# Gate products with the gate weights stationary, in one pipeline over the pairs of a half

## The chip, the cores and the metric

The kernel runs on one core of a Trainium2 chip. The metric is the device time of one execution in microseconds (us); lower is better. Before the change the median of 3 runs is 4451.63 us (4451.18 to 4458.18). The profiled execution took 4446.43 us, of which the span from the first to the last instruction is 4444.5 us. The engines are PE (TensorE), DVE (VectorE), ACT (ScalarE), POOL (GpSimd) and SP (SyncE, which here only issues DMAs).

## The reference

One graph layer on 12,500 nodes of 256 features: layer norm, a graph sum over 200,000 edges, linear attention, then a second layer norm and a top-2 mixture of 8 experts. The change concerns the gate of the last step:

```
x = x + gnn(xn) + mix(xn)                        # xn = layernorm(x)
x_flat = layernorm(x)
gate_logits = x_flat @ Wg + bg + bias            # (12500, 256) @ (256, 8)
topk_vals, topk_idx = top_k(gate_logits, 2)
topk_w = softmax(topk_vals)
h = relu(einsum('td,edh->teh', x_flat, W1) + b1)
y = einsum('teh,ehd->ted', h, W2) + b2
out = x + einsum('ted,te->td', y, combine)       # combine: topk_w at topk_idx
```

## The kernel before, in words

The nodes are 98 blocks of 128 rows (`NB`), handled as 49 pairs of blocks (`PAIRS`). A first stage sorts edges and projects the rows, a second gathers messages and adds them and the attention into `acc`, which stays in SBUF as 128 partitions x 98 blocks x 260 columns. Then comes the gate stage and after it the experts. The order of all work is written out by hand; the engines meet at semaphores.

**Gate stage.** The 49 pairs form 7 turns of 7 pairs (`TURN`, 14 blocks each, `TB`). Turns 0 to 2 are half 0 (21 pairs), turns 3 to 6 are half 1 (28 pairs). SP first stores every turn's rows of `acc` to `out` (`keep`, L578), then loads the experts' weights. For each pair:

- DVE normalises the two blocks in place (`normalise`, L1800). Between pairs it takes the statistics of the next turn's blocks (`block_stats`, L1771, 3 after each of the first four pairs and 2 after the fifth), gathers them (`gather_stats`, L1778 and L1780), and at the end of a turn inverts the standard deviation (`invert_turn`, L1786 to L1794), for which ACT has taken the root (`root`, L994).
- PE transposes the pair in 4 instructions into bank 0 or 1 (`f_transpose`, L1357), ACT copies the result to `fxn_t` (`gate_copies`, L1003), and PE multiplies (`gate`, L1365): the transposed rows are the stationary operand, 128 columns, and the gate weights `wg` are the moving one, 8 columns. The logits of a whole turn, tokens on the partitions, gather in bank 2.
- DVE reads bank 2 once a turn (`read_logits`, L1935), after the second pair of the next turn; PE may start the next turn's first product only when that is done (`s_gate_read`).

PE transposes a pair ahead: the order is transpose j, gate j-1. At a turn's end it does the gate of the last pair before the first transpose of the next turn.

After a half, DVE routes it (`route_half`, L1969 to L2060: best two experts, counts, positions) while PE counts tokens (`count_tokens`, L1386), and POOL then sends each block's rows twice to their experts' lists in DRAM (`send`, L772): 84 indirect DMAs for half 0, beside which half 1 goes through the gate. SP loads the first four units of the experts when half 0's sends have landed (L617). Half 1's sends (112) are issued beside the experts' first units.

**Experts.** Units of 256 rows: transposes (L1409), up (L1422), down (L1435) on PE, ACT and DVE between them, POOL adds the rows to `out` (L783). The second unit's up waits for the routing of half 1.

A float32 product is issued as two matmul instructions, a transpose as one, so a pair has 4 instructions of L1357 and 8 of L1365.

## Time and profile before

| | |
|---|---|
| median of the runs | 4451.63 us (4451.18 to 4458.18, n = 3) |
| profiled execution, its span | 4446.43 us, 4444.5 us |
| busy: PE, PE weight load, DVE, ACT, POOL | 3140.5, 2560.2, 2597.7, 604.6, 2537.1 us |
| mean granted clock of TensorE | 0.821 of full speed (its levels are 0.5 and 1) |
| gate stage (first normalised pair to the end of half 1's routing) | 3327.2 to 3599.8 us |
| gate products L1365, 392 instructions, mean | 349 ns |
| transposes L1357, 196 instructions, mean | 429 ns |

Times in all rows are microseconds from the span's start, but "mean ns". A slice of the page is 111 us. In a timeline row, the first number is the start, the second how long the group took, `x` the number of instructions, and the bracket the idle time of the engine before it with what ended it. "remote" and "issue" stand where the profile does not show what ended it. In the chain of waits each row is a piece of the chain that ended last. Ends of matmuls are modelled. In the stretches, "busy" is within the stretch, and the DMA share is the mean over the 16 DMA engines.

### The profile page before, as it was taken

What the parts mean: (1) busy time and instruction counts of PE and PEld (TensorE: products, weight loads), DVE (VectorE), ACT (ScalarE), POOL (GpSimd) and SP (SyncE); (2) the same over time, 40 slices, a digit from 0 to 9 for tenths busy, and PEclk for the clock granted to TensorE, in tenths of its full rate; (3) what the DMA queues carried; (4) which work ended last, traced back from release to release, by engine and by line L of the source; (5) the groups of instructions that cost most, each with busy time, mean ns of one, the idle gap of its engine ahead of it and who ended that gap; (6) DMA issues with size and microseconds to landing.
All of it is one profiled execution on the core that took longest, in us unless ns stands there. A gap on an engine that the chain in (4) does not pass through costs nothing.

```text
span 4444.5 us, 56780 instructions
## 1 busy us (share of the span) xinstructions
PE 3140.5 (71%) x16504; PEld 2560.2 (58%) x16505; DVE 2597.7 (58%) x6324; ACT 604.6 (14%) x1276; POOL 2537.1 (57%) x2437
## 2 busy tenths in 40 slices
PE   5767665566666666665676666666645379999998
PEld 5756554344545545544555555555535368888887
DVE  8887775444544544545767767667655145444444
ACT  8112221100000000000000000000001112222221
POOL 0057777466666666666666666666642447744444
PEclk9987777778778777778888888888875579999999
DMA  6666664533333333333333333333376235644443
GB/s 191 219 185 193 198 188 132 152 101 101 101 99 102 100 99 101 101 97 110 112 112 108 111 107 112 111 109 113 99 106 199 73 67 120 122 78 72 72 71 57
DMA packets 363112, 522.66 MB, mean 118 GB/s; under 512 B 69240, under 2 KB 282748, under 8 KB 363004
## 3 DMA queue, kind: packets, MB, share of 16 engines
q0 software_dynamic: 130944, 275.64, 25.7%
q1 hardware_dynamic: 181523, 190.28, 14.4%
q10 hardware_dynamic: 50537, 55.32, 4.0%
q8 instruction: 65, 1.06, 0.1%
q14 instruction: 43, 0.35, 0.0%
HBM read 378.21 MB, written 140.28 MB: 117 GB/s over the span
## 4 chain that ended last, share of the span: by engine, by line
PE 30%; another core or an unknown queue 17%; DVE 16%; issue 12%; DVEq 5%; DMA 2%; POOL 0%; ACT 0%; SPq 0%; ACTq 0%; POOLq 0%
PE bank L1422 9%; PE bank L1435 9%; DVE acc L1817 7%; PE bank L1230 6%; DVE select L1810 5%; DVEq L56 2%; PE bank L1333 2%; PE bank L1365 2%; DVEq L1817 1%; DVE relu_kq L1904 1%; PE bank L1409 1%; PE bank L1331 1%; DMA read_back<-lists 1%; PE bank L1357 1%
## 5 line engine op out<-in xcount | busy, mean ns | idle before, releaser
L729 POOL DMA_INDIRECT message<-h_table,gather_stage x1660 | 1583.3, 954 | 928.6 <-issue 505.9
L1817 DVE TENSOR_TENSOR acc<-acc,bank 128x256 f32 x1660 | 697.4, 420 | 880.5 <-remote 636.9
L1230 PE MATMUL bank<-message,select 128*128 128x256 f32 x3320 | 976.6, 449 | 294.5 <-issue 165.1
L1230 PEld LDWEIGHTS bank<-message,select 128*128 128x128 f32 x3320 | 726.2, 227 | 530.7 <-issue 245.7
L689 POOL DMA_INDIRECT lists<-placed,dest_i x300 | 374.3, 1248 | 375.7 <-ACT placed L911 281.2
L783 POOL DMA_INDIRECT out<-acc,row_of x224 | 351.3, 1568 | 341.3 <-DVE acc L2110 266.7
L1810 DVE TENSOR_SCALAR select<-iota_n,gather_stage 128x128 f32<-128x128 f32 x1660 | 467.3, 359 | 3.5
L1236 PE MATMUL bank<-w_cat,xt_in 128*128 128x256 f32 x784 | 257.1, 442 | 229.6 <-issue 228.7
L1422 PE MATMUL bank<-fx_t,acc 128*128 128x256 f32 x1792 | 411.8, 383 | 10.1 <-DVEq L2062 4.7
L1435 PE MATMUL bank<-w,acc 128*128 x1792 | 405.6, 379 | 2.7 <-issue 2.7
L1422 PEld LDWEIGHTS bank<-fx_t,acc 128*128 128x128 f32 x1792 | 344.9, 193 | 59.0 <-DVEq L2062 5.0
L1435 PEld LDWEIGHTS bank<-w,acc 128*128 128x128 f32 x1792 | 331.9, 190 | 43.8 <-issue 3.3
L1236 PEld LDWEIGHTS bank<-w_cat,xt_in 128*128 128x128 f32 x784 | 167.9, 216 | 289.1 <-issue 269.1
L772 POOL DMA_INDIRECT x_sorted<-acc,token_pos x196 | 191.4, 976 | 233.3 <-issue 148.4
L2106 DVE TENSOR_TENSOR acc<-bank,table 128x256 f32<-128x256 f32 x224 | 84.7, 419 | 315.0 <-PE bank L1435 258.6
L1331 PE MATMUL bank<-x_in,ident 128*128 128x256 f32 x196 | 102.7, 624 | 214.1 <-issue 120.9
L2094 DVE TENSOR_SCALAR acc<-bank,table 128x256 f32<-128x256 f32 x448 | 193.5, 478 | 67.2 <-PE bank L1422 43.3
L1331 PEld LDWEIGHTS bank<-x_in,ident 128*128 128x128 f32 x196 | 54.3, 304 | 245.0 <-issue 162.4
L1135 PE MATMUL bank<-hot_w,hot_q 128*128 128x128 bf16 x1575 | 157.3, 264 | 46.3 <-issue 44.7
L985 ACT ACTIVATE exp_kq<-bank 128x512 f32<-128x512 f32 x49 | 29.3, 597 | 1144.3 <-PE bank L1311 818.9
L1135 PEld LDWEIGHTS bank<-hot_w,hot_q 128*128 128x128 bf16 x1575 | 129.7, 121 | 68.6 <-issue 65.6
L963 ACT ACTIVATE exp_kq<-bank 128x512 f32<-128x512 f32 x49 | 29.3, 597 | 1027.0 <-remote 1027.0
(299 smaller groups left out, 3848.8 us busy)
## 6 DMA issues: line engine op xcount, KB each, us to landing
rows<-block_dram SPq DMA_DIRECT2D x75, 514.5 KB
acc<-x_sorted SPq DMA_DIRECT2D x112, 260.0 KB
message<-h_table,gather_stage POOLq DMA_INDIRECT x1660
xt_in<-xt_dram SPq DMA_DIRECT2D x98, 256.0 KB
x_sorted<-blank_rows ACTq DMA_DIRECT2D x42, 390.0 KB
lists<-zeros_list SPq DMA_DIRECT2D x8, 1664.0 KB, 15.4
read_back<-lists SPq DMA_DIRECT2D x13, 1024.0 KB, 5.7
x_sorted<-blank_rows SPq DMA_DIRECT2D x2, 6370.0 KB
```

The source lines that it names most:

```text
L689: pool.indirect_dma_start(out=lists, out_offset=Offset(ap=dest_i[:, c, i:i + 1], axis=0), in_=placed[:, c % 4, i * G8 * PIECES:(i + 1) * G ...
L729: pool.indirect_dma_start(out=message[:, slot % SETS, j, :], out_offset=None, in_=h_table, in_offset=Offset(ap=gather_stage[:, slot, j, 0: ...
L783: pool.indirect_dma_start(out=out, out_offset=Offset(ap=row_of[:, ring, j:j + 1], axis=0), in_=fy[:, slot, j, :], in_offset=None, compute_ ...
L1135: last = nc.tensor.matmul(bank[2 + c % 2][:, 0:P], hot_q[:, c % STEP, g, :], hot_w[:, c % STEP, g, :, :].rearrange("p r w -> p (r w)").bit ...
L1230: last = nc.tensor.matmul(ps, select[:, slot % 2, j, :], message[:, slot % SETS, j, :], start=True, stop=True)
L1236: last = nc.tensor.matmul(ps[:, u * C:(u + 1) * C], xt_in[:, half, k, u * P:(u + 1) * P], w_cat[:, k, cols:cols + C], start=(k == 0), stop ...
L1331: nc.tensor.matmul(bank[6][:, u * C:(u + 1) * C], ident[:, :], x_in[:, half, u, :], start=True, stop=False)
L1422: last = nc.tensor.matmul(bank[2 + 2 * slot + h // 2][:, h % 2 * 2 * P:(h % 2 + 1) * 2 * P], w1_now[:, slot, k * HID + h * P:k * HID + (h ...
L1435: last = nc.tensor.matmul(bank[6 + slot][:, j * C:(j + 1) * C], hid_t[:, slot, k, j * P:(j + 1) * P], w2_flat[:, ds(expert + k * C, C)], s ...
L1810: return V.tensor_scalar(select[:, slot % 2, j, :], iota_n[:, :], gather_stage[:, slot, j, 1:2].bitcast(F32), gather_stage[:, slot, j, 2:3 ...
L1817: added = V.tensor_tensor(to, to, ps, ALU.add)
L2094: last = V.tensor_scalar(hid_t[:, slot, h, :], bank[2 + 2 * slot + h // 2][:, h % 2 * 2 * P:(h % 2 + 1) * 2 * P], table_flat[:, ds(expert ...
```

## The change

The gate product is turned round: the gate weights are stationary (8 columns) and the transposed rows move (256 columns), so that a pair's logits come out with the 8 experts on the partitions, in bank 3 or 6. ACT copies them to the new tile `logit_t` (four buffers), and PE turns them back with two transposes (`gate_back`) into the turn's bank, 2 or 7 in alternation. The pairs of a half form one pipeline on PE: transpose g, product g-1, turn back g-2, without a break at turns. ACT's loops over turns are written out. On DVE the next turn's statistics come after the first three pairs of a turn (5, 5 and 4), the gathering after the third, and the read of the last turn's logits after the fourth pair. ACT takes the root in the third pair of a turn.

```diff
--- before.py
+++ after.py
@@ -288,6 +288,7 @@
         xtile_f = sb("xtile_f", [P, 1], F32, route)
         xtile_i = sb("xtile_i", [P, 2, 1], I32, route)
         fxn_t = sb("fxn_t", [P, 2, KC, 2 * P], F32, route)
+        logit_t = sb("logit_t", [EXPERTS, 4, 2 * P], F32, route)
         newton_turn = sb("newton_turn", [P, TB], F32, route)
         route.close()
 
@@ -379,6 +380,8 @@
         s_table = sem("s_table")
         s_kept = [sem(f"s_kept{i}") for i in range(TURNS)]
         s_fin = sem("s_fin")
+        s_logit_psum = sem("s_logit_psum")
+        s_logit = sem("s_logit")
         s_gate = sem("s_gate")
         s_gate_read = sem("s_gate_read")
         s_route = sem("s_route")
@@ -991,18 +994,28 @@
 
             def root(turn):
                 act.wait_ge(s_var, turn + 1)
-                act.activation(rstd[:, ds(turn * TB, TB)], row_mean[:, ds(turn * TB, TB), 1], ACT.Sqrt,
+                act.activation(rstd[:, turn * TB:turn * TB + TB], row_mean[:, turn * TB:turn * TB + TB, 1], ACT.Sqrt,
                                bias=eps_col[:, :]).then_inc(s_std, 1)
 
-            def gate_copies(turn, first=False, last=False):
-                for j in range(TURN):
-                    g = turn * TURN + j
-                    act.wait_ge(s_xt_psum, g + (PAIRS + 1))
-                    if not first or j > 1:
-                        act.wait_ge(s_gate, g if j == 0 else g - 1)
-                    act.activation(fxn_t[:, j % 2, :, :].rearrange("p k n -> p (k n)"), bank[j % 2][:, :], ACT.Identity).then_inc(s_xt, 1)
-                    if j == TURN - 3 and not last:
-                        root(turn + 1)
+            def gate_copies(half):
+
+                first, end = HALF_BEGIN[half], HALF_BEGIN[half] + HALF_PAIRS[half]
+
+                def copy_logits(g):
+                    act.wait_ge(s_logit_psum, g + 1)
+                    if g >= 4:
+                        act.wait_ge(s_gate, g - 3)
+                    act.activation(logit_t[:, g % 4, :], bank[3 + 3 * (g % 2)][0:EXPERTS, 0:2 * P], ACT.Copy).then_inc(s_logit, 1)
+                for g in range(first, end):
+                    act.wait_ge(s_xt_psum, PAIRS + g + 1)
+                    if g >= 2:
+                        act.wait_ge(s_logit_psum, g - 1)
+                    act.activation(fxn_t[:, g % 2, :, :].rearrange("p k n -> p (k n)"), bank[g % 2][:, :], ACT.Identity).then_inc(s_xt, 1)
+                    if g > first:
+                        copy_logits(g - 1)
+                    if g % TURN == 2 and g // TURN + 1 < TURNS:
+                        root(g // TURN + 1)
+                copy_logits(end - 1)
 
             def softmax_exp(half):
 
@@ -1010,13 +1023,9 @@
                 blocks = slice(HALF_BEGIN[half] * 2, (HALF_BEGIN[half] + HALF_PAIRS[half]) * 2)
                 act.activation(top_w[:, 1, blocks], small[:, 4, 0:2 * HALF_PAIRS[half]], ACT.Exp).then_inc(s_route, 1)
             root(0)
-            gate_copies(0, first=True)
-            with act.Fori(1, TURNS_1) as m:
-                gate_copies(m)
+            gate_copies(0)
             softmax_exp(0)
-            with act.Fori(TURNS_1, TURNS - 1) as m:
-                gate_copies(m)
-            gate_copies(TURNS - 1, last=True)
+            gate_copies(1)
             softmax_exp(1)
 
 
@@ -1347,36 +1356,49 @@
 
             pe.wait_ge(s_fin, 48)
 
-            def f_transpose(g, j, first=False):
+            def f_transpose(g):
                 pe.wait_ge(s_fxn, g + 1)
-                if not first:
-
-                    pe.wait_ge(s_xt, g + (PAIRS if j == 0 else PAIRS - 1))
+                if g >= 2:
+                    pe.wait_ge(s_xt, PAIRS + g - 1)
                 for k in range(KC):
                     for u in range(2):
-                        last = nc.tensor.transpose(bank[j % 2][:, (k * 2 + u) * P:(k * 2 + u + 1) * P],
+                        last = nc.tensor.transpose(bank[g % 2][:, (k * 2 + u) * P:(k * 2 + u + 1) * P],
                                                    acc[:, g * 2 + u, k * P:(k + 1) * P], ident[:, :])
                 last.then_inc(s_xt_psum, 1)
 
-            def gate(g, j):
-                pe.wait_ge(s_xt, g + (PAIRS + 1))
+            def gate(g):
+
+                pe.wait_ge(s_xt, PAIRS + g + 1)
+                if g >= 2:
+                    pe.wait_ge(s_logit, g - 1)
+                for k in range(KC):
+                    last = nc.tensor.matmul(bank[3 + 3 * (g % 2)][0:EXPERTS, 0:2 * P], wg[:, k, :], fxn_t[:, g % 2, k, :],
+                                            start=(k == 0), stop=(k == KC - 1))
+                last.then_inc(s_logit_psum, 1)
+
+            def gate_back(g):
+
+                turn, j = g // TURN, g % TURN
+                pe.wait_ge(s_logit, g + 1)
+                if j == 0 and turn >= 2:
+                    pe.wait_ge(s_gate_read, turn - 1)
                 for u in range(2):
-                    for k in range(KC):
-                        last = nc.tensor.matmul(bank[2][:, (j * 2 + u) * EXPERTS:(j * 2 + u + 1) * EXPERTS],
-                                                fxn_t[:, j % 2, k, u * P:(u + 1) * P], wg[:, k, :],
-                                                start=(k == 0), stop=(k == KC - 1))
+                    at = (j * 2 + u) * EXPERTS
+                    last = nc.tensor.transpose(bank[2 + 5 * (turn % 2)][:, at:at + EXPERTS],
+                                               logit_t[:, g % 4, u * P:(u + 1) * P], ident[0:EXPERTS, 0:EXPERTS])
                 last.then_inc(s_gate, 1)
 
-            def gate_turn(turn, first=False):
-
-                g = turn * TURN
-                for j in range(TURN):
-                    f_transpose(g + j, j, first and j < 2)
-                    if j == 1 and not first:
-                        pe.wait_ge(s_gate_read, turn)
-                    if j:
-                        gate(g + (j - 1), j - 1)
-                gate(g + (TURN - 1), TURN - 1)
+            def gate_half(half):
+                first, end = HALF_BEGIN[half], HALF_BEGIN[half] + HALF_PAIRS[half]
+                for g in range(first, end):
+                    f_transpose(g)
+                    if g > first:
+                        gate(g - 1)
+                    if g > first + 1:
+                        gate_back(g - 2)
+                gate(end - 1)
+                gate_back(end - 2)
+                gate_back(end - 1)
 
             def count_tokens(half):
 
@@ -1386,12 +1408,9 @@
                     last = nc.tensor.matmul(ps[:, 0:cols * EXPERTS], matrix[:, :],
                                             both_bf[:, 0:cols, :].rearrange("p b e -> p (b e)"), start=True, stop=True)
                 last.then_inc(s_route_psum, 1)
-            gate_turn(0, first=True)
-            for turn in range(1, TURNS_1):
-                gate_turn(turn)
+            gate_half(0)
             count_tokens(0)
-            for turn in range(TURNS_1, TURNS):
-                gate_turn(turn)
+            gate_half(1)
             count_tokens(1)
 
 
@@ -1933,19 +1952,19 @@
             def read_logits(turn, half):
                 dve.wait_ge(s_gate, turn * TURN + TURN)
                 V.tensor_copy(logits[:, turn * TB - 2 * HALF_BEGIN[half]:turn * TB - 2 * HALF_BEGIN[half] + TB, :].rearrange("p b e -> p (b e)"),
-                              bank[2][:, 0:TB * EXPERTS]).then_inc(s_gate_read, 1)
+                              bank[2 + 5 * (turn % 2)][:, 0:TB * EXPERTS]).then_inc(s_gate_read, 1)
 
             def gate_turn(turn, half, read=True):
 
                 dve.wait_ge(s_kept[turn], 32 if turn == TURNS - 1 else 16)
                 for j in range(TURN):
                     normalise(turn * TURN + j)
-                    if read and j == 1:
+                    if read and j == 3:
                         read_logits(turn - 1, half)
-                    if turn < TURNS - 1 and j < TURN - 2:
-                        for b in range(j * 3, min(j * 3 + 3, TB)):
+                    if turn < TURNS - 1 and j < 3:
+                        for b in range(j * 5, min(j * 5 + 5, TB)):
                             block_stats(turn * TB + TB, b)
-                    if turn < TURNS - 1 and j == TURN - 3:
+                    if turn < TURNS - 1 and j == 2:
                         gather_stats(turn * TB + TB)
                 if turn < TURNS - 1:
                     invert_turn(turn + 1)
```

What stands in a row, first on PE where turn 0 ends. Before, the piece shows the last pairs of turn 0 and the first of turn 1 (`bank0`, `bank1`: transposed rows; `bank2`: logits; moving operand first, then stationary):

```order
L1357 MATMUL bank1<-ident,acc 128x128 x4
L1365 MATMUL bank2<-wg,fxn_t 128x8 x4
L1357 MATMUL bank0<-ident,acc 128x128 x4
L1365 MATMUL bank2<-wg,fxn_t 128x8 x8
L1357 MATMUL bank0<-ident,acc 128x128 x4
L1357 MATMUL bank1<-ident,acc 128x128 x4
L1365 MATMUL bank2<-wg,fxn_t 128x8 x4
```

The last product of the turn stands ahead of the next transposes. After the change the same place reads:

```order
L1387 MATMUL bank2<-ident,logit_t 128x8 x2
L1365 MATMUL bank0<-ident,acc 128x128 x4
L1375 MATMUL bank6<-fxn_t,wg 8x256 x2
L1387 MATMUL bank2<-ident,logit_t 128x8 x2
L1365 MATMUL bank1<-ident,acc 128x128 x4
L1375 MATMUL bank3<-fxn_t,wg 8x256 x2
L1387 MATMUL bank7<-ident,logit_t 128x8 x2
```

There is no break at the turn; each pair has its transposes, the product of the pair before and the turn back of the one before that, which goes over from bank 2 to bank 7.

On DVE, turn 1, from its first normalised pair (`acc`), through the statistics (BN_STATS), before:

```order
L1800 TENSOR_SCALAR acc<-acc,row_mean,rstd 128x256 x2
L1771 BN_STATS stats<-acc 128x6 x3
L1800 TENSOR_SCALAR acc<-acc,row_mean,rstd 128x256 x2
L1935 COPY logits<-bank2 128x112
L1771 BN_STATS stats<-acc 128x6 x3
L1800 TENSOR_SCALAR acc<-acc,row_mean,rstd 128x256 x2
L1771 BN_STATS stats<-acc 128x6 x3
L1800 TENSOR_SCALAR acc<-acc,row_mean,rstd 128x256 x2
L1771 BN_STATS stats<-acc 128x6 x3
L1800 TENSOR_SCALAR acc<-acc,row_mean,rstd 128x256 x2
L1771 BN_STATS stats<-acc 128x6 x2
L1776 MEMSET turn_mark 128x1
```

The gathering follows this piece, then the last two pairs and the inversion. After the change, from the same first pair on:

```order
L1819 TENSOR_SCALAR acc<-acc,row_mean,rstd 128x256 x2
L1790 BN_STATS stats<-acc 128x6 x5
L1819 TENSOR_SCALAR acc<-acc,row_mean,rstd 128x256 x2
L1790 BN_STATS stats<-acc 128x6 x5
L1819 TENSOR_SCALAR acc<-acc,row_mean,rstd 128x256 x2
L1790 BN_STATS stats<-acc 128x6 x4
L1795 MEMSET turn_mark 128x1
L1797 BN_AGGR turn_stats<-stats 128x2 x14
L1799 COPY row_mean<-turn_stats 128x28
L1819 TENSOR_SCALAR acc<-acc,row_mean,rstd 128x256 x2
L1954 COPY logits<-bank2 128x112
L1819 TENSOR_SCALAR acc<-acc,row_mean,rstd 128x256 x6
```

The statistics and their gathering have moved into the first three pairs, the read of the logits from the second pair to the fourth, and the last three pairs stand in a row.

## Rows read from the trace of the kernel before

**Rows 1.** The page's slices: granted clock of TensorE in tenths, 40 slices of the span.

```profile
PEclk9987777778778777778888888888875579999999
```

**Rows 2.** Three stretches: start:end, us, busy (instructions) by engine, clock, DMA share, GB/s.

```profile
3328.15:3381.40 53.25, 52.70 (x252) 51.61 (x252) 33.56 (x147) 14.41 (x25) 0.00 (x0) 0.50 1.04 346
3426.00:3521.00 95.00, 6.47 (x28) 5.57 (x27) 3.10 (x11) 1.20 (x2) 64.19 (x67) 0.50 0.30 105
3521.50:3574.80 53.30, 50.98 (x244) 50.25 (x244) 25.60 (x108) 19.29 (x28) 0.00 (x0) 0.50 0.00 1
```

**Rows 3.** The chain of waits in half 0: start, us, what.

```profile
3332.23 0.95 PE bank L1357 x4
3333.18 1.51 PE bank L1365 x8
```

**Rows 4.** Timeline of DVE in half 0.

```profile
3327.19 0.74 DVE L1800 TENSOR_SCALAR acc<-acc,row_mean,rstd 128x256 f32<-128x256 f32 x2
3327.84 1.07 DVE L1771 BATCH_NORM_STATS2 stats<-acc 128x6 f32<-128x256 f32 x3
3328.83 0.72 DVE L1800 TENSOR_SCALAR acc<-acc,row_mean,rstd 128x256 f32<-128x256 f32 x2
...
3335.13 0.18 DVE L1778 BATCH_NORM_AGGREGATE turn_stats<-stats 128x2 f32<-128x6 f32 x1
...
3336.28 1.38 DVE L1800 TENSOR_SCALAR acc<-acc,row_mean,rstd 128x256 f32<-128x256 f32 x4
3338.94 0.24 DVE L1786 RECIPROCAL rstd<-rstd 128x14 f32<-128x14 f32 x1 [1.29 <-ACT rstd L994]
...
3340.05 0.74 DVE L1800 TENSOR_SCALAR acc<-acc,row_mean,rstd 128x256 f32<-128x256 f32 x2
```

**Rows 5.** Timeline of DVE: the last read of logits of each half.

```profile
3381.40 0.27 DVE L1935 COPY logits<-bank 128x112 f32<-128x112 f32 x1 [6.22 <-PE bank L1365]
...
3574.81 0.27 DVE L1935 COPY logits<-bank 128x112 f32<-128x112 f32 x1 [14.05 <-PE bank L1365]
```

**Rows 6.** Timeline of ACT beside the sends: copies of pairs 26, 27 and 28.

```profile
3450.07 0.60 ACT L1003 ACTIVATE fxn_t<-bank 128x512 f32<-128x512 f32 x1 [24.41 <-remote]
3483.67 0.60 ACT L1003 ACTIVATE fxn_t<-bank 128x512 f32<-128x512 f32 x1 [33.00 <-remote]
...
3522.73 1.08 ACT L1003 ACTIVATE fxn_t<-bank 128x512 f32<-128x512 f32 x2
```

**Rows 7.** Timeline of PE beside the sends: transposes of pairs 28 and 29.

```profile
3486.05 1.95 PE L1357 MATMUL bank<-ident,acc 128*128 128x128 f32 x8
```

**Rows 8.** Timelines of POOL and SP: first and last send, loads of units.

```profile
3403.54 1.05 POOL L772 DMA_INDIRECT x_sorted<-acc,token_pos  x1 [81.54 <-DVE acc L1800]
...
3509.34 0.97 POOL L772 DMA_INDIRECT x_sorted<-acc,token_pos  x1 [0.30 <-issue]
...
3511.82 1.91 SPq L617 DMA_DIRECT2D acc<-x_sorted  x4
```

**Rows 9.** The chain of waits in the experts' first units.

```profile
3599.83 5.80 PE bank L1422 x16
...
3629.97 0.44 PE bank L1409 x4
3630.41 3.46 PE bank L1435 x16
```

**Rows 10.** Timeline of PE in the sorting stage.

```profile
260.63 2.40 PE L1135 MATMUL bank<-hot_w,hot_q 128*128 128x128 bf16 x21
262.83 1.06 PE L1146 MATMUL bank<-ident,x_buf 128*128 128x128 f32 x4
```

**Rows 11.** The same place in two stretches.

```profile
262.00:266.00 4.00, 3.58 (x30) 3.23 (x29) 2.29 (x9) 0.00 (x0) 3.08 (x4) 0.52 0.14 41
266.00:270.00 4.00, 1.55 (x10) 1.14 (x8) 3.97 (x6) 1.95 (x5) 1.54 (x2) 0.91 0.27 64
```

**Rows 12.** The stores of line 578 from issue to landing.

```profile
DMA to landing us min/median/max: 6.9/13.9/16.1
```

## The prediction

> **What bounds the kernel now.** I read the page's slices first, then the chain of waits around the gate stage, then each engine's timeline there, and last the queues. The granted clock of TensorE is at its lower level, 0.5, in two slices of 111 us, from 3333 on [rows 1]. That is the gate stage, from 3327 to 3600 us of the 4444.5 us span; nothing outside it is edited. It has four parts.
>
> Half 0 (21 pairs) lasts from 3327.2 to 3381.4. PE is busy in 52.7 of 53.25 us, at clock 0.50, while DVE is busy in 33.6 [rows 2]. The chain alternates 0.95 us of transposes and 1.51 us of gate products, 2.46 us a pair [rows 3]. So PE sets this part, and DVE waits for it.
>
> Routing half 0 on DVE runs from 3381.4 to the first send at 3403.5 [rows 5, 8].
>
> Half 1 runs beside 84 sends of POOL, one every 1.27 us, from 3403.5 to 3509.3 [rows 8]. From about 3411 to 3521 almost nothing moves: in 95 us PE is busy 6.5, DVE 3.1, ACT 1.2, and the 16 DMA engines only 30% [rows 2]. ACT copies pair 26 at 3450.07 and pair 27 at 3483.67, 33.6 us later; PE starts the transposes of 28 and 29 at 3486.05, and ACT can copy them only at 3522.7 [rows 6, 7]. The transposes are thus recorded on time, and their completion reaches ACT 35 us late. One pair is 4 transposes and 8 gate product instructions (each float32 product is two), so 33.6 us is 2.8 us per PE instruction. The slowness ends when the sends and the four unit loads behind them (issued from 3511.8) are through, at 3521.4. I take it as a price on PE's completions beside back-to-back sends: it comes and goes with them, and in half 0, with the DMA engines full and no send, it isn't there.
>
> What is left of half 1, 21 pairs, takes from 3521.4 to 3574.8, again with PE busy (51.0 of 53.3 us) at clock 0.50 [rows 2, 5]. Routing half 1 then takes 25.0 us up to 3599.8, where the experts go on [rows 5, 9]. From there to the end PE is full, so what the gate stage gains or loses arrives at the end unchanged.
>
> **The change part by part, PE.** A pair's 8 instructions with 128 stationary and 8 moving columns go. In come 4 with 8 stationary and 256 moving columns, and 2 small transposes. At the upper clock a 128x256 float32 product takes 3.46/16 = 0.216 us and four transposes 0.44 us [rows 9]. Four products are 0.86. For the turn back no row has the price: it can't be under two transposes' spacing, 0.22, since it loads as many stationary columns, nor over two of the old gate instructions at the lower clock, 2 x 0.19 = 0.38 [rows 3]; I take 0.3. A pair is 0.44 + 0.86 + 0.3 = 1.6 us at the upper clock. At the lower one the transposes are 0.95, the products 4 x 0.43 = 1.73 and the turn back 0.38: 3.06 us, 0.6 more than today's 2.46.
>
> **Which clock.** This decides the sign. What PE did before a rise can be read: in the sorting stage it ran 21 products of 128 columns, then four 128x128 transposes, and the clock went from 0.52 in 262 to 266 to 0.91 in the next 4 us [rows 10, 11]; of the experts' 128x256 products, the 16 from 3599.8 on take 5.80 us and those at 3630.4 take 3.46 [rows 9]. In the old gate stage PE is as busy, yet two thirds of its instructions move 8 columns, and the clock stays down. The new pair moves 256 columns in four of its ten instructions and 128 in four more, about as dense as the sorting stretch. So I expect the upper level within a few us of each half's start.
>
> The Trainium skill (TensorE: Matmul & The Clock Gate, Part 4: PE-mode transpose) says that transposes don't count as activity for the clock. By it only the products would speak for a rise, and it might not come; that is the first rival. The sorting rows do not settle it, since products stand on both sides of the transposes.
>
> **DVE.** It issues what it issued, in another order, and no longer waits for the square root (1.29 us a turn). Per turn: 7 pairs normalised at 0.65, 14 statistics at 0.99/3 = 0.33, the gathering 1.15, the inversion 1.11 [rows 4], a read of logits about 0.2: 4.5 + 4.6 + 1.15 + 1.1 + 0.2 = 11.6 us. PE wants 7 x 1.6 = 11.2. So DVE becomes the bound by a little in full turns. The read of logits moved to the fourth pair needs the last turn's pairs turned back; they are by then, as PE lies about two pairs behind. In the first three pairs DVE delivers one per 2.3 us, and PE works off its backlog meanwhile.
>
> **ACT.** 49 copies of 8x256 are added, each below the 0.60 of the 128x512 copy [rows 6]; taken as 0.4, ACT has 1.0 us of work in a pair of 1.6. PE asks for a copy one pair later, so it hides; if it did not, 0.4 us x 49 = 20 us would be the worst. The loops become straight code, and some table loads go; worth under 2 us.
>
> **The stores.** DVE may not normalise a turn before its rows are stored. SP issues the turns' stores one behind the other as soon as `acc` is complete, ahead of the weights' loads, and they land 6.9 to 16.1 us after issue [rows 12]; turn 2's is the third of them, and DVE asks for it at 3350 instead of 3361. Nothing, or a few us if it were late.
>
> **Sum.** Half 0: two turns of 11.5 (the first reads no logits) from 3327.2 end at 3350.2. In the third, three pairs with statistics and the gathering take 7.7, the fourth is normalised at 3358.5, PE does four pairs by 3364.9, and the last product, its copy and turn back add 1.9: 3366.8 instead of 3381.4, -14.6. With some us at the lower clock first, -12 to -15.
>
> The sends then start and end 14.6 earlier, and so does the slow stretch: 3506.8 instead of 3521.4. In it, at 2.8 us for each of 10 instructions, a pair takes 28 us, so 110 us hold 3.9 pairs instead of 3.3. But DVE now brings the first pairs of the half one per 2.3 us instead of 1.6, so PE enters the stretch with one to two pairs fewer. I take 22 pairs left instead of 21. If the price belongs to stationary columns, a pair is 6 x 2.8 = 17 us and about 19 are left.
>
> After it: 22 x 1.6 = 35.2, 2 for the tail, 2.5 for a start at the lower clock: 39.7 instead of 53.4, -13.7. DVE is ahead, having far less than that to do. Routing is unchanged.
>
> Together -28.3: the profiled execution's 4446.4 becomes 4418. The median of the runs is 4451.6, 5.2 above the profile, so I predict 4423. Its own range is 4412 to 4434: the turn back +-3.5, the clock's start +-3, pairs left +-5.
>
> **Rivals.** (a) The clock stays at 0.5: slower. Place: both stretches in which PE sets the pace. Price: 3.06 instead of 2.51 us a pair (17.55 a turn by the chain's 7 x 2.46 and 0.35 at its seam), 21 x 0.55 = 11.5 in half 0; after the slow stretch 22 x 3.06 + 2 = 69.3 against 53.4, 15.9. Sum +27: 4479. For it: 270 us of clock 0.5 with a busy PE [rows 1, 2] and the page's rule; against it: the columns moved. It decides once the mean pair costs over 2.5 us, that is if the upper clock holds less than about a third of the time. 14 in 100.
>
> (b) The sends no longer slow PE, or far less: it needs the slowness to come from the 128-column loads or from the old handing over. Half 1 then ends by about 3440, its routing by 3465, and the experts start when the sends and loads are through, near 3505 to 3512, 88 us earlier than 3599.8: 4363. Against it: transposes pay the price too, and they stay. The Trainium skill (SBUF — State Buffer, Who interferes with whom) says that DMA never contends with a compute engine and that PE waits on no one; by it the slowness would not be the sends' doing at all. The rows show that it begins and ends with them. 5 in 100.
>
> (c) The gain is eaten: PE pays in the slow stretch per handing over (three signals a pair instead of two, 50 us a pair), ACT's extra copies show, or the clock flips in each turn's sparse first pairs. With 24 pairs left, 2.0 us a pair and no gain from the first 3 pairs of turns, half 0 gives -6 and the rest 24 x 2.0 + 2 = 50, -3: 4443, at the edge of no change. 13 in 100.
>
> The forecast has 68. A measurement tells this kernel from no change beyond 0.2%, 8.9 us. Faster: all of the forecast, (b), and a third of (c), 0.77; same, 0.08; slower (a) and a little of (c), 0.15. The range, 4400 to 4452, covers the forecast and (c).
>
> **What would show it.** Granted clock near 1 in 3335 to 3367; DVE busy nearly throughout, 11.6 us a turn; first send near 3389; ACT's copies 28 us apart in the slow stretch; last read of logits near 3546; experts on at 3571. I am wrong if the clock in half 0 reads 0.5, if turns take over 14 us, or if the stretch beside the sends has another length than some 107 us plus the loads.

## The result and the profile after

The changed kernel takes 4422.44 us in the median of 3 runs (4421.71 to 4427.46), the kernel before 4451.63: ratio 0.9933 (95% interval 0.9911 to 0.9956). Predicted were 4423, in a range of 4400 to 4452. That the two agree to a microsecond is partly luck: four terms of the sum were off by some 3 us each and nearly cancelled, and on another Trainium2 chip the same change gives half as much, as the experiments show.

The span of the profiled execution is 4425.5 us against 4444.5. The gate stage begins 9.7 us later in it (first normalised pair at 3336.85, before at 3327.19 [rows 4]), because the message stage ahead of it, whose code the change does not touch, ended later in this execution. So each part is measured from that row on. Parts of the stage, first before, then after:

| part | before, us | after, us | change | predicted |
|---|---|---|---|---|
| half 0: first normalised pair to last read of logits | 54.2 | 42.8 | -11.4 | -14.6 |
| routing of half 0, to the first send | 22.1 | 22.2 | +0.1 | 0 |
| first send to the end of the slow stretch | 117.9 | 117.6 | -0.3 | 0 |
| from there to the last read of logits | 53.4 | 37.0 | -16.4 | -13.7 |
| routing of half 1, to the experts' second unit | 25.0 | 25.1 | +0.1 | 0 |
| together | 272.6 | 244.6 | -28.0 | -28.3 |

The three stretches of [rows 2], now in the changed kernel (columns as there: busy time of the engines, granted clock, DMA share, GB/s):

```profile
3336.85:3379.62 42.77, 40.44 (x210) 19.98 (x210) 34.20 (x149) 21.41 (x46) 0.00 (x0) 0.89 1.03 350
...
3424.00:3519.00 95.00, 12.03 (x38) 5.11 (x36) 2.83 (x18) 3.28 (x7) 64.72 (x67) 0.50 0.30 106
3519.50:3556.50 37.00, 35.98 (x194) 17.70 (x194) 19.66 (x78) 20.40 (x44) 0.00 (x0) 0.94 0.00 1
```

The page's clock, one digit per slice of 111 us, answers to [rows 1]: one slice at 5 is left of two.

```profile
PEclk9987777877777777777878878888877589999999
```

The clock is up in the first and third (0.50 before), and PE is still busy nearly throughout them: it stays the bound. PE's timeline at the start of half 0:

```profile
3340.96 1.88 PE L1375 MATMUL bank<-fxn_t,wg 128*8 128x256 f32 x4
3342.77 1.12 PE L1365 MATMUL bank<-ident,acc 128*128 128x128 f32 x4
3343.82 1.88 PE L1375 MATMUL bank<-fxn_t,wg 128*8 128x256 f32 x4
3345.62 0.38 PE L1387 MATMUL bank<-ident,logit_t 8*128 8x8 f32 x2
...
3349.52 0.66 PE L1365 MATMUL bank<-ident,acc 128*128 128x128 f32 x4
3350.11 1.03 PE L1375 MATMUL bank<-fxn_t,wg 128*8 128x256 f32 x4
3351.07 0.29 PE L1387 MATMUL bank<-ident,logit_t 8*128 8x8 f32 x2
3351.28 0.66 PE L1365 MATMUL bank<-ident,acc 128*128 128x128 f32 x4
```

In these rows the last figure of `128*8` or `128*128` is the number of stationary columns. Starts give the pace. With the clock down, 3340.96 to 3343.82 is 2.86 us, without the turn back's 0.3; with it up, 3349.52 to 3351.28 is 1.76 us a pair: 0.59 of transposes, 0.96 of products, 0.21 of turning back. The upper level holds from about 3346 on. Without it the change would lose, by the same rows: 2.86 and 0.3 us a pair stand against 2.46 before [rows 3].

DVE's last reads of the two halves, which answer to [rows 5]: the 7.37 and 8.32 us ahead of them are waits for PE, as DVE has normalised everything by then.

```profile
3379.62 0.28 DVE L1954 COPY logits<-bank 128x112 f32<-128x112 f32 x1 [7.37 <-PE bank L1387]
...
3556.42 0.28 DVE L1954 COPY logits<-bank 128x112 f32<-128x112 f32 x1 [8.32 <-PE bank L1387]
```

The chain of waits in the slow stretch (start, length, what):

```profile
3444.62 11.15 another core or an unknown queue
3455.82 16.75 another core or an unknown queue
3472.62 10.45 another core or an unknown queue
3483.12 16.76 another core or an unknown queue
3499.93 11.17 issue
```

Each piece ends at a copy of ACT, at 3455.82 of logits and at 3472.62 of the next transposed pair. So 10.45 to 11.2 us go by for 4 products, and 16.75 for 4 transposes and 2 turns back: 2.6 to 2.8 us per instruction, though products load 8 stationary columns and transposes 128. ACT has copied 8 transposed pairs of the half when the stretch ends, so 20 are left; before it had copied 7, the last at 3483.67 [rows 6], and 21 were left. The experts' second unit, which answers to [rows 9], starts at 3581.47 (before 3599.83).

### The profile page after: what moved, and what is told of

Read it like the earlier page. It is cut to its first block, busy times and chain, and to the rows that moved or that the text cites. A ratio compares the mean times of both kernels' runs of the same rounds, so it can differ in the third digit from the quotient of the medians.

```text
span 4425.5 us, 56657 instructions
## 1 busy us (share of the span) xinstructions
PE 3128.6 (71%) x16406; PEld 2500.9 (57%) x16407; DVE 2600.6 (59%) x6324; ACT 616.6 (14%) x1320; POOL 2538.0 (57%) x2437
## 4 chain that ended last, share of the span: by engine, by line
PE 30%; DVE 17%; another core or an unknown queue 15%; issue 13%; DVEq 5%; DMA 1%; POOL 1%; ACT 0%; SPq 0%; POOLq 0%
PE bank L1441 9%; PE bank L1454 9%; DVE acc L1836 8%; PE bank L1239 6%; DVE select L1829 5%; DVEq L56 2%; PE bank L1342 2%; DVEq L1836 1%; DVE relu_kq L1923 1%; PE bank L1428 1%; PE bank L1375 1%; PE bank L1340 1%; DMA read_back<-lists 1%; DVEq L57 1%
```

## The experiments

The experiments ran on four chips, which are of two kinds: on three of them (the fast kind) the kernel before took 3966 to 3970 us, on one (the slow kind) 4477, and the first measurement, 4451.63, belongs with the latter. Each chip was used only once, in one group of runs, so it is not shown that the kind is a lasting property of the chip and not a condition that it was in. Each run is compared with the kernel before on its own chip, and a stage within one trace. "Half 0" is again the time from the first normalised pair to the last read of its logits.

**The order of DVE alone (chip with 3969 us).**

```
-   if turn < TURNS - 1 and j < TURN - 2:  # range(j * 3, j * 3 + 3)
+   if turn < TURNS - 1 and j < 3:         # range(j * 5, j * 5 + 5)
-   ... j == TURN - 3 (gathering; ACT's root)
+   ... j == 2
```

> The kernel before, with the change's DVE order alone (statistics 5, 5, 4 after the first three pairs of a turn, the gathering after the third, ACT's root in the third pair); gate product and bank as before. Theory (PE at the lower clock sets the pace): half 0 stays at 54 us within 1, the granted clock at 0.5, the time within 4 us of before. Rival (the order of DVE carries a part of the gain): half 0 shorter by 3 us or more, the time 5 to 10 us below before.

Ratio 1.0002 (0.9993 to 1.0012); half 0 takes 55.5 us, ACT's copies are 2.46 apart. The order alone gives nothing: PE's pace hides it. The kernel before was not profiled on a chip of the fast kind, so this run stands for it below.

**The new gate with DVE's old order (3969 us).** The diff is the reverse of the one above, in the changed kernel, with the read of logits after the second pair.

> The changed kernel with DVE's order of before (statistics 3, 3, 3, 3, 2, the gathering after the fifth pair, logits read after the second, the root in the fifth pair). Theory: with PE at 1.76 us a pair (12.3 a turn) DVE's 11.6 plus 1.3 of waiting for the root is 12.9 a turn, so half 0 takes 1 to 3 us more than with the change and what follows the slow stretch is unchanged: 1 to 4 us over the changed kernel. Rival (the order carries half of the gain once PE is fast): 10 us or more over it.

Ratio 0.9987 (0.9978 to 0.9997), against 0.9968 for the whole change (below). Half 0 takes 48.3 us, 5.8 more than with the new order (42.5), where I expected 1 to 3 more. The trace of DVE shows why:

```profile
2948.66 0.24 DVE L1805 RECIPROCAL rstd<-rstd 128x14 f32<-128x14 f32 x1 [1.14 <-ACT rstd L997]
...
2955.33 0.28 DVE L1954 COPY logits<-bank 128x112 f32<-128x112 f32 x1 [3.20 <-PE bank L1387]
...
2985.39 0.28 DVE L1954 COPY logits<-bank 128x112 f32<-128x112 f32 x1 [3.84 <-PE bank L1387]
```

A turn loses not only the root's 1.1 us but 3.2 in which DVE stands in front of logits that PE has not turned back yet; the next pairs then come late to PE. There is a second loss: PE stands idle for 1.99 us before the fourth pair of turns 1 and 2, and the granted clock falls to 0.50 for a while (2957.2 to 2960.7 and 2974.3 to 2977.7); the pair in the first of these takes 3.17 us in place of 1.76. The order is worth nothing under the slow gate and nearly half of half 0's gain under the fast one: 55.5, 48.3 and 42.5 us.

**More moving columns beside the old products (3969 us).**

```
+   nc.tensor.matmul(bank[6][0:EXPERTS, 0:2 * P], wg[:, 0, :], fxn_t[:, j % 2, 0, :], start=True, stop=True)
    for u in range(2):      # the old gate products follow
```

> The kernel before with one product added to each pair, whose result nobody reads: gate weights stationary, 256 columns of fxn_t moving, two PE instructions. The old gate products stay. Theory (the old products' 8 moving columns kept the clock down; more moving columns raise it): granted clock near 1 in most of half 0; a pair is 0.59 of transposes, 8 x 0.1 of old products and 0.48 of the added one, 1.87 us in place of 2.46; half 0 43 to 46 us, after the slow stretch 41 to 45, the slow stretch at 14 instructions a pair 39 us a pair; together 15 to 24 us below before. Rival (the orientation of the product, not the clock, is what helped): the clock stays at 0.5, a pair is 2.46 + 0.86 = 3.3 us, half 0 70 us, together some 35 us above before.

Ratio 1.0062 (1.0037 to 1.0088): my theory fell. A pair takes 3.71 us where the rival said 3.3, and the clock stays down with PE busy all the time:

```profile
2940.00:3004.00 64.00, 64.00 (x242) 43.46 (x240) 24.15 (x105) 11.47 (x22) 0.00 (x0) 0.50 0.81 257
```

With a product of 256 moving columns added to each pair and the eight instructions of 8 moving columns kept, the clock did not rise. What it is in the old products that keeps it down, their few moving columns or something else, no run separates. The cost arrives in full: from the first normalised pair to the first unit's transposes it is 27 us more than in the run with DVE's order alone (218.1 against 191.1), and the kernel is 26.9 us over the one before.

**Transposes alone (3966 us).** The products are left out, so no logits are computed.

```
-   matmul(bank[3 + 3 * (g % 2)][0:EXPERTS, 0:2 * P], wg[:, k, :], fxn_t[:, g % 2, k, :])   # k = 0, 1
+   transpose(bank[3 + 3 * (g % 2)][:, ...], fxn_t[:, g % 2, k, u * P:(u + 1) * P], ident)  # k, u = 0, 1
```

> The changed kernel with its 4 product instructions a pair (256 moving columns each) replaced by 4 more 128x128 transposes of fxn_t: the logits are not computed, and in the gate stage PE runs transposes alone. Theory (transposes raise the clock as products do): granted clock near 1 after the first pairs of half 0, a pair 1.3 to 1.5 us, DVE sets the pace at 11.5 a turn, half 0 37 to 40 us. Rival (transposes do not count for the clock): it stays at 0.5 in half 0, a pair is 2 x 1.09 + 0.3 = 2.4 to 2.5 us, half 0 53 to 56 us.

The clock rises, in a stretch in which PE runs nothing but transposes. Two stretches of it, then PE's timeline about the rise:

```profile
2936.02:2949.00 12.98, 9.73 (x43) 7.88 (x44) 12.73 (x54) 4.65 (x10) 0.00 (x0) 0.52 1.04 350
2949.00:2968.00 19.00, 15.21 (x122) 12.75 (x123) 18.67 (x86) 10.97 (x27) 0.00 (x0) 1.00 1.02 332
```

```profile
2946.81 1.11 PE L1365 MATMUL bank<-ident,acc 128*128 128x128 f32 x4
...
2948.88 0.66 PE L1365 MATMUL bank<-ident,acc 128*128 128x128 f32 x4
...
2950.12 0.66 PE L1365 MATMUL bank<-ident,acc 128*128 128x128 f32 x4
```

PE's last product ahead of this stretch starts at 2924.70, and PE then stands idle for 11 us. A pair takes 1.24 us, DVE sets the pace at 11.5 to 11.7 a turn, half 0 takes 39.9 us, and the kernel 3956.03 (one run). The clock does fall back once, from 2969.0 to 2972.5, after PE had stood idle for 0.92 and 1.93 us, waiting for DVE. The Trainium skill (TensorE: Matmul & The Clock Gate, Part 4: PE-mode transpose) says that transposes do not count as activity for the clock; this run, with transposes in float32, disagrees, and the measurement decides. The rival that rested on it had no ground.

**The change itself on such a chip (3966 us).** No edit.

> The changed kernel itself, beside the kernel before on one chip. In the first four runs the kernel before took 3968.6 us in place of 4451.6, half 1 of the gate ran at full pace beside the sends, and the first unit of the experts started when the sends and the loads behind them were through. Theory (there only what comes ahead of the first send counts; half 1 is hidden beside 107 us of sends): on such a chip the change gives 11 to 13 us, the shortening of half 0, and nothing of half 1: ratio 0.997. On a chip where ACT's copies beside the sends are 28 us apart: 26 to 30 us, ratio 0.9935. Rival (half 1 counts on both): 25 us or more on either.

Ratio 0.9968 (0.9957 to 0.9978): 12.7 us by the ratio and 13.7 between the medians, not 29. POOL's first and last send of half 0 and PE's first transposes of the experts, changed kernel:

```profile
2992.06 1.05 POOL L775 DMA_INDIRECT x_sorted<-acc,token_pos  x1 [69.84 <-DVE acc L1819]
...
3099.40 0.97 POOL L775 DMA_INDIRECT x_sorted<-acc,token_pos  x1 [0.30 <-issue]
...
3105.40 1.09 PE L1428 MATMUL bank<-ident,acc 128*128 128x128 f32 x4 [48.05 <-DMA acc<-x_sorted]
```

Half 1 runs beside the sends at full pace (from 2995 to 3046 PE is busy 49.6 of 51 us, clock 0.98), and PE then waits 48 us for the sends and the load behind them. Only what lies ahead of the first send counts: first normalised pair to first unit 178.0 us against 191.1 with the old gate (the run with DVE's order alone), 13.1 less.

**Every second send left out (3966 us).** Each row reaches one expert's list only; SP and ACT wait for half as many landings.

```
-   for i in range(4 * HALF_PAIRS[0]):
+   for i in range(0, 4 * HALF_PAIRS[0], 2):
```

> The changed kernel with every second send of half 0 left out (42 in place of 84; each row goes to one expert's list only). Theory (the sends set when the first unit starts): the last send is 53 us earlier and the first unit starts some 53 us earlier; then half 1's gate and routing are the later ones: on a chip with full pace beside sends the second unit starts 77 us after the first pair of half 1, in all 35 to 45 us below the changed kernel. On a chip with the slow stretch it is 53 us shorter, two pairs more are left behind it, some 48 us below. Rival (the stage is set by half 1, not by the sends): less than 5 us.

3916.42 us (one run), 36 below the changed kernel. The first unit's transposes start 130.0 us after the first normalised pair in place of 178.0, and the second unit now waits for routing:

```profile
3078.80 6.52 PE L1441 MATMUL bank<-fx_t,acc 128*128 128x256 f32 x16 [5.71 <-DVEq L2081]
```

It starts 143.5 us after the first normalised pair in place of 187.8. The cover of half 1 is thus gone after 44 of the 53 us; of these, 7.9 don't show in the total, since in this execution the gate stage began that much later.

**Sends held back until half 1 is through (one chip of each kind).**

```
    pool.wait_ge(s_fxn, HALF_PAIRS[0])
+   pool.wait_ge(s_gate, PAIRS)
```

> The changed kernel in which POOL sends half 0's first block only when the gate products of half 1 are all turned back. Theory (the sends back to back make PE's completions late): no slow stretch; half 1 goes through at 1.76 us a pair, 50 us from the routing of half 0 on, its routing follows at once; the sends take 107 us behind it, the unit loads 12 more, and the first unit's products start about 171 us after the first pair of half 1 in place of 169, the second unit's at once behind it: 3 to 10 us below the changed kernel. Rival (the slowness belongs to half 1's work or to the stretch of time and not to the sends): half 1's gate still takes 100 us or more and the time is about 100 us above the changed kernel's.

> Again the changed kernel in which POOL sends half 0's first block only when half 1 is turned back. On a chip where the kernel before takes 3970 us: 43 us above it, as in the first run. On a chip where it takes 4450: if the slow stretch belongs to the sends, half 1 goes through in 50 us and the kernel takes 5 to 12 us less than the changed one; if PE's completions are late there whatever POOL does, half 1 takes 100 us or more without a send, and the kernel some 100 us more.

On the chip with 3969 us: ratio 1.0106 (1.0088 to 1.0124), 43 us slower, since there the sends are the long part and were only put off. On the one with 4477 us it takes 4451.75 (one run), and its trace shows what the slow stretch needs. Half 1 in that run, then the stretch of the sends:

```profile
3426.00:3478.00 52.00, 51.23 (x276) 25.35 (x276) 36.46 (x158) 28.60 (x60) 0.00 (x0) 0.95 0.00 1
3482.00:3590.00 108.00, 0.93 (x2) 0.13 (x2) 19.49 (x57) 0.41 (x2) 82.56 (x84) 0.50 0.29 103
```

Without sends, the chip that is slow beside them does 28 pairs in 52 us. So the slow stretch needs the sends and a chip of this kind; neither alone makes it. The sum was wrong, though. The changed kernel itself was not run on this chip; the nearest is the one with a warm start (below), 4447.6 in a range of 4441.8 to 4454.8, and this one is not 5 to 12 us under it. In the traces, the experts' fifth up product starts 279.0 us after the first normalised pair, and 274.3 with the warm start. The timeline of the experts' first units shows why:

```profile
3594.31 5.82 PE L1442 MATMUL bank<-fx_t,acc 128*128 128x256 f32 x16 [0.78 <-issue]
...
3599.96 0.60 PE L1429 MATMUL bank<-ident,acc 128*128 128x128 f32 x4
...
3614.15 0.60 ACT L1037 ACTIVATE fx_t<-bank 128x512 f32<-128x512 f32 x1 [19.04 <-remote]
...
3614.89 5.76 PE L1442 MATMUL bank<-fx_t,acc 128*128 128x256 f32 x16 [14.33 <-ACT fx_t L1037]
```

POOL goes straight on from the 84 sends to the first 12 of half 1, and the transposes recorded at 3599.96 reach ACT 13.6 us late. Such a wait is not new: it stands in the runs without the hold too, where the same 12 sends are issued beside the experts. The changed kernel of the first trace has PE idle for 7.45 us ahead of the up products at 3605.89. The run with the warm start has this:

```profile
3613.73 0.60 PE L1430 MATMUL bank<-ident,acc 128*128 128x128 f32 x4
...
3620.11 0.60 ACT L1036 ACTIVATE fx_t<-bank 128x512 f32<-128x512 f32 x1 [11.54 <-remote]
...
3620.99 4.32 PE L1443 MATMUL bank<-fx_t,acc 128*128 128x256 f32 x16
```

There the transposes reach ACT 5.8 us late. With the sends held back the wait is longer and stands ahead of the second unit, 14.33 us of PE. So what the hold won was lost, at least in part, in a longer wait behind it.

**A warm start (4477 us).**

```
+   for i in range(56):
+       nc.tensor.transpose(bank[7][:, i % 4 * P:(i % 4 + 1) * P], ident[:, :], ident[:, :])
    pe.wait_ge(s_fin, 48)
```

> The changed kernel with 56 transposes of the identity (128x128, into bank 7, read by nobody) between PE's last aggregation and the gate, where PE otherwise waits 11 us for DVE. Theory (PE's transposes alone raise the clock, and half 0 begins at the lower one only because PE stood still): granted clock near 1 from the first pair, the first three pairs at 1.8 in place of 2.9 us; the last logits of half 0 are read 2 to 4 us earlier after the first normalised pair (42.8 to 43.3 before), and the first send likewise: 2 to 4 us below the changed kernel, some 16 below the kernel before (ratio 0.996). Rival (DVE's one pair per 2.3 us in the first three pairs hides it): half 0 unchanged within 1 us, ratio 0.997.

Ratio 0.9935 (0.9918 to 0.9953), as for the change without it; half 0 takes 42.4 us against 42.2 in the run above. The time is the rival's, but its reason was not tested, as half 0 did not begin at the upper clock. The clock rises at about 3346, after PE's last products and the first 1.6 us of the transposes; the transposes end after 7.1 us, PE waits 4.28 us for DVE, and the clock falls at about 3356, as the first pair's transposes end. PE's timeline, then four stretches:

```profile
3344.30 7.08 PE L1358 MATMUL bank<-ident 128*128 128x128 f32 x56
3355.65 0.63 PE L1367 MATMUL bank<-ident,acc 128*128 128x128 f32 x4 [4.28 <-DVE acc L1821]
```

```profile
3346.00:3350.00 4.00, 4.00 (x38) 4.00 (x38) 3.70 (x12) 0.00 (x0) 2.06 (x10) 1.00 0.42 148
3350.00:3354.00 4.00, 1.38 (x13) 1.14 (x11) 3.52 (x25) 0.31 (x1) 0.00 (x0) 1.00 1.04 324
3354.00:3358.00 4.00, 0.79 (x5) 0.58 (x6) 3.86 (x14) 0.60 (x1) 0.00 (x0) 0.77 1.04 358
3358.00:3362.00 4.00, 4.00 (x13) 1.74 (x14) 3.96 (x21) 1.13 (x3) 0.00 (x0) 0.50 1.04 349
```

More transposes, up to DVE's first pair, would have asked the question; this was not run. As half 0 is no shorter with this warm start, the ratio can be read as that of the change on a chip of the slow kind, and it agrees with the first (0.9933).

**Sends one by one with the pairs of half 1 (3966 and 3970 us).**

```
    for i in range(4 * HALF_PAIRS[0]):
+       if i < HALF_PAIRS[1]:
+           pool.wait_ge(s_gate, HALF_PAIRS[0] + i + 1)
        send(0, i)
```

> The changed kernel in which each of the first 28 sends of half 0 waits for one more pair of half 1 to be turned back; the other 56 follow back to back. Theory for a chip with full pace beside sends: 28 sends at 1.76 us in place of 1.27 and the first one 4 us later, 15 to 20 us above the changed kernel. For a chip with the slow stretch: if only sends back to back make PE's completions late, half 1 goes through in 50 to 60 us, then 56 sends in 71 us, 30 to 45 us below the changed kernel; if any send does, pairs come 28 us apart and the kernel takes several hundred us more.

> Again the changed kernel with each of the first 28 sends of half 0 waiting for one more pair of half 1. On a chip where the kernel before takes 3970: 20 us above the changed kernel, as in the first run. On one where it takes 4450 to 4480: if only sends back to back make completions late, half 1 goes through in 50 to 60 us beside them and the kernel takes 15 to 45 us less than the changed one; if any send does, at a pair per send each pair waits 20 us or more, and the kernel takes several hundred us more.

3976.38 and 3983.78 us (one run each): the first is 24 over the changed kernel, the second 23 over the variant below, which ran on the same chip. That is a little more than the 15 to 20 worked out: in the first of them 27 intervals between sends take 46.7 us in place of 34.7, and the first send comes 8 us later after the first normalised pair, as it waits for a pair to be turned back. Both runs met chips of the fast kind, so what was asked of the slow kind is open.

**Fewer sends ahead of the experts' first unit (3970 us).**

```
-   AHEAD, SPREAD = 12, 42
+   AHEAD, SPREAD = 2, 42
```

> The changed kernel with AHEAD = 2 in place of 12: of half 1's sends only two stand ahead of the first unit's rows, the rest are spread over the units as before. Theory for a chip where the kernel before takes 4450 to 4480 (sends back to back make PE's completions late): the stall of the experts' third unit, 7 to 14 us some 15 us behind the first of the 12 sends, goes; 5 to 12 us below the changed kernel, ratio 0.991 to 0.992. Rival (the stall is one of the first units, not of the sends): ratio 0.9935 as the changed kernel. On a chip where the kernel before takes 3970 no stall is there to take away: ratio 0.997, as the changed kernel.

Ratio 0.9972 (0.9962 to 0.9982), as for the change alone. No stall is there to take away on this kind of chip; whether it goes on the other was not seen. No version that computes everything beat the changed kernel.

## Why the prediction held, step by step

**The clock rises in both halves.** Right, about 9 us after the first pair in half 0 and 4 us after the release in half 1. My reason, columns moved, was too coarse: the run with one wide product added kept the clock down. The rule of the Trainium skill on transposes (TensorE: Matmul & The Clock Gate, Part 4: PE-mode transpose), a ground of rival (a), does not hold in the run with transposes alone.

**A pair at 1.6 us, DVE the bound at 11.6 a turn.** Wrong: the pair takes 1.76, so a turn of PE is 12.3 and PE stays the bound. Transposes cost 0.59 up to the start of what follows (0.44 taken from rows where products of 128 stationary columns follow), products 0.96 (0.86 taken), the turn back 0.21 (0.3 taken, and 0.22 called its floor). DVE's turns are 11.5 and 11.7, as worked out. Two pairs at the lower clock, 2.85 and 3.16 us, come on top, and half 0 gave -11.4 and not -14.6. The sum was right for a PE faster than DVE: in the run with transposes alone half 0 takes 39.9 us, and the sum had 39.6.

**The slow stretch: same length, 2.8 us per instruction, 28 us a pair.** Right to 3% (27.3 to 28.0 between ACT's copies), and by instructions, not stationary columns. The price came from one interval of 33.6 us, though; the one before it, 26.6 us from 3423.44 to 3450.07, would have given 2.2 us. What I took as a general price of sends beside PE is one of this kind of chip: on three others it is absent. The Trainium skill (SBUF — State Buffer, Who interferes with whom) says that PE waits on no one. On the fast kind nothing here speaks against it. On the slow kind PE's instructions beside the sends take as long as elsewhere at the lower clock (four products 1.87 us, four transposes 1.11); what comes late is the signal that they are done, of which that sentence does not speak. How the sends delay it is not shown.

**22 pairs left.** Wrong by two: DVE's slower delivery of the first pairs did not matter, since the fourth copy of ACT comes at 3410.66 and came at 3411.19 before. 20 were left, 20 x 1.76 = 35.2, which is by luck also 22 x 1.6; start and tail took 1.8 and not 4.5: 37.0 and not 39.7. So the errors of +3.2 in half 0 and -2.7 here nearly cancelled.

**ACT hides its extra copies.** Right: 0.37 us each, and ACT stands 0.43 and 0.36 us idle in every pair of 1.76.

**What was missing** is that the larger part of the gain needs the slow stretch. Of -28.0 us, 16.4 are earned behind it; where half 1 is not held up it hides beside the sends, and 12.7 us are left. The forecast was made from a trace of the slow kind and measured on one; it names nothing that would tell the kinds apart, and on the other it would have been some 15 us too low.

## What to carry to other kernels

Work out a gain per stage, then ask under which other work that stage would lie if the machine behaved a little better; half of this gain existed only behind a stall. A new order for one engine can be worth nothing alone and nearly half of a stage's gain once the engine ahead of it is faster (half 0: 55.5 us with the order alone, 48.3 with the new gate alone, 42.5 with both), so try the parts together and apart. Before delaying work to free another engine, look at what is issued right behind it: with the sends held back, a wait of 14.33 us stood ahead of the experts' second unit.

## What the hardware showed

Trainium2 chips differ: the same kernel takes 3966 to 3970 us on three and 4452 to 4477 in two other measurements, with the same instructions at the same recorded durations (a copy 0.60, a send 0.97). In the gate stage the difference is that PE's completions come late beside indirect DMAs. That is the smaller part of it: of the 477.5 us between the two traces of the changed kernel, 409 lie ahead of the gate, where from 800 to 2400 us POOL issues 1051 indirect DMAs against 1267 and the mean clock is 0.78 against 0.91; the cause there was not looked for. The traces of the slow kind also hold less than half as many recorded semaphore events (23,520 against 56,590 for the changed kernel). So their "remote" rows can hide a releaser, and it is not shown that the delay exists without the profiler, which recorded every run here.

PE's transposes raised its clock from 0.52 to 1.00 without any product. And the clock, once up, can be lost before the work begins: after the warm start PE waited 4.28 us, did one pair's transposes in 0.63 us and waited again, and the next stretch reads 0.50.
